# Graph convolution and routed feed-forward on one core: one more wait of GpSimd per half of 16 gathers

## What is computed

```python
def _gcn_layer(x, W, b, edge_weight, edge_src, edge_dst):
    support = x @ W
    msgs = support[edge_src] * edge_weight[:, None]
    agg = jax.ops.segment_sum(msgs, edge_dst, num_segments=N_NODES)
    return agg + b
...
h = jax.nn.elu(_gcn_layer(layernorm(x), W1, b1, ...))
h = jax.nn.elu(_gcn_layer(h, W2, b2, ...))
x = x + h
...
xf = layernorm(x)
H = jax.nn.gelu(xf @ W1 + b1, approximate=False)
probs = jax.nn.softmax(H @ Wg + bg, axis=-1)
assign = jnp.argmax(probs, axis=-1)
out = sum over e of where(assign == e, probs[:, e:e + 1] * (H @ Wd[e] + bd[e]), 0.0)
x = x + out
```

## Time and profile before

| | |
|---|---|
| timed runs, median of 3 | 4540.26 us (4538.99 to 4540.56) |
| profiled execution, its span | 5639.2 us |
| profiled execution, its own time | not given apart from the span |
| TensorE (PE) busy | 3611.2 us, 64% of the span, 21407 instructions |
| VectorE (DVE) busy | 2125.6 us, 38% |
| ScalarE (ACT) busy | 1218.9 us, 22% |
| GpSimd (POOL) busy | 3287.1 us, 58%, 3464 instructions |
| mean granted clock of TensorE | 0.741 of full |

### The profile page before, as it was taken

The page is one execution under the profiler, slowest core; times in us unless marked ns, Lnnn a source line. Parts: engine busy times, 40 slices in busy tenths (PEclk is TensorE's granted clock), DMA queues, the critical chain, the costliest instruction groups (busy, mean ns, idle before and its releaser), DMA issues.

```text
span 5639.2 us, 84567 instructions
## 1 busy us (share of the span) xinstructions
PE 3611.2 (64%) x21407; PEld 3303.4 (59%) x21408; DVE 2125.6 (38%) x7215; ACT 1218.9 (22%) x2041; POOL 3287.1 (58%) x3464
## 2 busy tenths in 40 slices
PE   4555445555555545557667676666776776678998
PEld 3554444555544545456666666666666666667777
DVE  6663233223232322224334443333443433354332
ACT  4551110000000000013223232232232322232111
POOL 5666556666666666655565655555555555524555
PEclk6666666666666666668777777778777777789999
DMA  4543323333333333323333333333333333344444
GB/s 149 166 154 92 90 86 91 95 96 93 96 95 96 94 96 93 94 77 103 104 115 113 114 114 114 106 108 111 113 112 110 111 111 104 107 130 142 156 156 138
DMA packets 248031, 626.81 MB, mean 111 GB/s; under 512 B 66279, under 2 KB 113014, under 8 KB 247358
## 3 DMA queue, kind: packets, MB, share of 16 engines
q0 software_dynamic: 173664, 491.88, 30.3%
q1 hardware_dynamic: 69646, 103.75, 5.1%
q10 hardware_dynamic: 4176, 26.61, 1.3%
HBM read 519.22 MB, written 103.73 MB: 110 GB/s over the span
## 4 chain that ended last, share of the span: by engine, by line
PE 40%; issue 24%; another core or an unknown queue 4%; DVEq 4%; DVE 3%; DMA 2%; ACT 1%; POOL 0%; POOLq 0%; ACTq 0%; SPq 0%
PE pA L1381 18%; PE pB L1422 13%; PE pZ L1391 3%; PE pC L1404 3%; DMA aggT<-pay_scratch,ids 2%; PE pA L1536 1%; DVE S L927 1%; DVEq L927 1%; PE pZ L1415 1%; DVEq L953 1%; PE pT L1410 0%; DVE aggT L978 0%; PE pC L1526 0%; DVEq L978 0%
## 5 line engine op out<-in xcount | busy, mean ns | idle before, releaser
L1381 PE MATMUL pA<-S,rows 128*128 128x96 f32 x12544 | 1857.1, 312 | 961.7 <-issue 639.8
L1381 PEld LDWEIGHTS pA<-S,rows 128*128 128x128 f32 x12544 | 1797.0, 228 | 1039.1 <-issue 1033.8
L549 POOL DMA_INDIRECT rows<-h_scratch,idx x1564 | 1491.4, 954 | 1107.8 <-issue 424.2
L549 POOL DMA_INDIRECT rows<-xn_scratch,idx x1296 | 1227.9, 947 | 742.7 <-issue 366.2
L1422 PE MATMUL pB<-work,w 128*128 128x128 f32 x3232 | 776.5, 380 | 707.3 <-issue 702.3
L1422 PEld LDWEIGHTS pB<-work,w 128*128 128x128 f32 x3232 | 656.0, 279 | 818.9 <-issue 818.2
L927 DVE TENSOR_SCALAR S<-iota_p,tdst,twgt 128x96 f32<-128x96 f32 x3168 | 852.8, 351 | 288.2 <-issue 280.7
L978 DVE TENSOR_TENSOR aggT<-aggT,pA 128x192 f32 x784 | 278.0, 355 | 1340.3 <-remote 851.1
L1030 DVE TENSOR_TENSOR zb<-pZ,brow 128x256 f32<-128x256 f32 x198 | 84.0, 424 | 1150.0 <-issue 692.8
L1391 PE MATMUL pZ<-wg,stage 128*128 128x256 f32 x784 | 276.0, 485 | 213.0 <-ACT stage L642 126.2
L1536 PE MATMUL pA<-aggT,work 128*128 x1680 | 387.5, 384 | 10.8 <-DVE work L1311 10.1
(11 more groups left out here) (200 smaller groups left out, 2613.9 us busy)
## 6 DMA issues: line engine op xcount, KB each, us to landing
pay_scratch<-work SPq DMA_DIRECT2D x98, 512.0 KB
rows<-h_scratch,idx POOLq DMA_INDIRECT x1564
rows<-xn_scratch,idx POOLq DMA_INDIRECT x1296
work<-in_x_dram ACTq DMA_DIRECT2D x15, 896.0 KB
xn_scratch<-work ACTq DMA_DIRECT2D x14, 896.0 KB
h_scratch<-work SPq DMA_DIRECT2D x98, 128.0 KB
pay_scratch<-work SPq DMA_DIRECT2D x98, 128.0 KB
work<-in_x_dram SPq DMA_DIRECT2D x97, 128.0 KB
```

What stands on the lines that cost most here:

```text
L549: pool.indirect_dma_start(rows[:, s, t, :], None, source, bass.IndirectOffsetOnAxis(at, 0))\
L1381: last = mm(to[:, k * W:(k + 1) * W], rows[:, slot, t, k * P:(k + 1) * P], Sx[:, t, :], start=(t == 0), stop=(t == T - 1))
```

## The change

Ahead of the waits for indices and for a slot, each half but the first of a layer now waits for `s_gath` of the last slot of the half before it (slot 7 for an even half, slot 3 for an odd one), at the value that the four gathers of this slot bring it to. `landed` gives this value: each half adds 4 x 16 to the slot's semaphore, and each slot is used once in two halves, so it is 32 h for even h and 32 h + 32 for odd h; what the padded first half has less is taken off.

```diff
+            def landed(h, half):
+
+                times = h * (8 * T)
+                return times if half == 0 else times + 8 * T
+
             def gathers(layer, source, h, quarter, first=False):
 
                 half = quarter % 2
+                if not first:
+                    before = (1 - half) * HALF + HALF - 1
+                    hold(pool, s_gath[layer][before], landed(h, half) - 16 * FEWER[before])
                 for u in range(HALF):
                     s = half * HALF + u
                     if u == 0:
```

## The result

The change takes 5048.44 us (median of 4 runs, 5044.86 to 5049.75) against 4539.77 us before (4 runs, 4538.99 to 4540.56). The ratio is 1.1118, its 95% interval 1.1102 to 1.1133: 508.7 us more, 2.62 us for each of the 194 added waits. Forecast were 4969 us in a range of 4800 to 5070. Direction, cause and range were right; the point was 79 us low, and the measured time is 22 us under the range's upper end.

A forecast was written before the change was run, and what follows sets the result against it. GpSimd's own gather pitch was taken to bound both layers. Each wait adds 1.70 landing + 0.81 starting again - 0.30 idle time already there = 2.21 us; 194 waits add 429 us to 4540: 4969 us, range 4800 to 5070.

The forecast's parts named there:

- The sum of 4604 us: Floor without stalls: 3128 gathers x 1.25 = 3910 us, 21 ahead, 25.3 between the layers, end of 647.5.
- the profile adds: Claim that the profile's 1099 us over the timed runs sits in TensorE's "issue" time, absent unprofiled.
- starting again: At each added wait, GpSimd's time from the rows' landing to its next gather: 0.81 us, low 0.27.
- Landing: At each added wait, time from the last gather's instruction end until its rows land: 1.70 us, plain 1.58, long 2.49.
- the contention with the stores of layer 2: In layer 2, 512 KB stores meet a landing one time in eight, making it 2.49 us instead of 1.58.
- The wait is hidden: GpSimd already waits for a free slot at each half's head, so time stays at 4540 us; chance 0.09.
- Half hidden: TensorE is late in layer 2 alone; only layer 1 pays, 97 x 2.21 = 214 us, 4754 us; chance 0.06.
- TensorE becomes the bound: Longer pauses lower TensorE's clock to 0.66 in layer 2: 69 us more, 5038 us; chance 0.04.
- Faster: Fewer gathers in flight leave the stores of layer 2 alone, giving a gain; chance 0.01.
- The idle time at the heads: Sign: 2.5 us idle ahead of each half's first gather, ending with "DMA rows".
- the pitch inside a half: Sign: gathers inside a half stay 1.25 us apart.
- a profiled span of 5640 to 5800: Sign: the changed kernel's profiled span grows far less than 429 us, as waits for a free slot shrink.

## Why the prediction was right, and what was off

**What bounds it** was read rightly, with one wrong reason. The argument was that 3128 gathers at 1.25 us and the rest make more than the timed 4540 us, so no stall of GpSimd can be in it. Its conclusion held: the changed kernel's profile has the pitch of 1.25 us throughout, both layers at the same 22.6 to 22.7 us a half, and TensorE early. The sum of 4604 us was above the time because its end (647.5 us) and its gap between the layers (25.3 us) came from the slower pace; at the pace of the result they are 577.9 and 16.6, and the sum is 4525 (4533 with the mean pitch). The wrong reason was "the profile adds": the profiler adds nothing, the profiled execution ran at the other pace.

**The term that was too small** is "starting again". The prediction took 0.81 us and said of the added register and semaphore instructions that nothing is put down for them. Measured are 1.12 us from the landing to the start of the gather, 1.10 in the mean. The 0.81 was right for a wait that stands last (0.80 in that run); the 0.3 us were missing for the waits for indices and slot, which stand behind the new one with their register instructions. While GpSimd works, such instructions are free; behind a wait that stops it, each is on the path, 0.15 us for the first and 0.32 for both. In the means, a head has 2.95 us where 2.51 were foreseen, 0.29 from the restart and 0.16 from the landing. Over 194 waits that is 86 us of idle time, of which 79 show in the time; the rest is as little as the sums above can tell.

**Landing.** 1.86 us in the mean against 1.70. Both parts of the term were off, and in part they made up for each other: the plain landing, 1.58, read from the last slice with traffic, is 1.79 in the median of layer 1 and at no head under 1.70, and the contention with the stores of layer 2, put at 0.11 us, shows as 0.05 (a mean of 1.88 us there against 1.83 in layer 1). The estimate by the Trainium skill's "DMA: Bandwidth & Descriptors", section "Anatomy of one DMA — SWDGE (gpsimd) path", 2.3 us from issue to landing, is below the 2.6 that the trace has as its least.

**The rivals.** *The wait is hidden* did not come, at the pace of the result; at the other it is mostly what happens (509 us become 141 to 157). *Half hidden* had the place wrong: where the wait is hidden, it is so more in layer 1 than in layer 2, 19 against 122 us. *TensorE becomes the bound* did not come, as TensorE waits for rows in 513 places. The clock is 0.58 in layer 1 and 0.81 in layer 2 where the profile ahead of the prediction has 0.66 and 0.76, but that one is of the other pace; at the same pace the changed kernel has 0.65 and 0.75, so the change has hardly moved it. *Faster* did not come.

**What was to be seen.** The idle time at the heads, the pitch inside a half: yes. The label was "issue" in place of "DMA rows". The end at 647 us and a profiled span of 5640 to 5800: not in the profile of the result, which has 577.9 and 5047; in the profiles at the second pace they are 645.6 us, and 5776.7 and 5807.6.

**Open.** What makes this program run at one pace or the other (whether it is the chip is not shown: chips 6, 7, 8 and 12 had the second, and the chip of the result isn't on record); what the stretches of 0.70 us are; why, at the second pace, one wait per half costs 141 to 157 us and two cost nothing. The traces say only that the "issue" stretches of TensorE ahead of that product grow with one (691.7 to 765.8 and 799.7 us) and go with two (82.3 us). The fetching of instructions moves the same packets at either pace, 532 or 533 of them in its DMA queue, which neither supports nor excludes that they arrive late. No version that beats the kernel before at its faster pace came out of this.

## What to carry to other kernels

Add up the pacemaker's own work without any stall before believing the stalls in its profile: where that sum equals the time, each microsecond of wait put into its stream is paid in full, here 2.6 us for a wait on the DMA just issued. A wait for the group of transfers before that cost nothing, though this was run only where the engine had slack. A wait that will stop the engine costs least behind those that will not: 0.3 us less idle time each, which no time of a run here has confirmed (of the two kernels with the wait moved, one took as long as the change within the noise, the other 75 us longer). And when a profile's span and the timed runs differ by a quarter, find out whether they ran at the same pace before ascribing the difference to the profiler.

## What the runs showed of the hardware that was not expected

- The same program has two paces, 4540 and 5590 to 5690 us, and all timed runs of one measurement are of one of them; the first varies by 0.04% from run to run (0.1% with the change), the second by some 1% around its median. In the second, TensorE and VectorE have stretches in which instructions start 0.70 us or a multiple apart while nothing is waited for; GpSimd's gathers keep their 1.25 us.
- At the second pace less work can be slower: a quarter of the products gives 5865 us in place of 5613, and twice the waits 5620 in place of 5776.
- A gather of 128 rows of 1 KB lands 2.6 to 3.6 us after its start where the view has it (median 2.7), at the heads 1.8 us after its instruction's end in the median. From there to the start of the next gather pass 1.12 us with two more waits in between, 0.95 with one and 0.80 without.
